# Per-batch statistics one step of attention later, expert weights awaited piece by piece, in a two-layer gated cross-attention and mixture-of-experts kernel

## The chip, the core and the metric

One Trainium2 chip; the kernel runs on one core. The metric is the device time of one execution in microseconds (us). Engines are called PE (TensorE; PEld its weight loads), DVE (VectorE), ACT (ScalarE), POOL (GpSimd) and SP (SyncE, which here issues transfers only).

## The reference, cut to what matters

Two layers, each of cross-attention and a feed-forward part with shared and routed experts. x is 4 batches of 512 tokens by 512; the context has the same tokens by 128. Attention has 32 query heads of 16 columns in 8 groups, one key and value head each. Layer 0 routes to 2 of 8 experts of width 256, layer 1 to 6 of 32 experts of width 192.

```python
def _L0_xattn_ref(q, k, v):            # _L1_xattn_ref computes the same
    QH, KVH = (32, 8); D = E // QH; G = QH // KVH
    qh = q.reshape(b, s, KVH, G, D).transpose(0, 2, 3, 1, 4)
    kh = k.reshape(b, s, KVH, D).transpose(0, 2, 1, 3)
    vh = v.reshape(b, s, KVH, D).transpose(0, 2, 1, 3)
    scores = jnp.einsum('bkgsd,bktd->bkgst', qh, kh) * scale
    attn = jax.nn.softmax(scores, axis=-1) / DROPOUT
    out = jnp.einsum('bkgst,bktd->bkgsd', attn, vh)
...
def _L1_ffn_ref(hidden_states, gate_w, wg, wu, wd, sg, su, sd):
    scores = jax.nn.sigmoid(x @ gate_w)
    topk_w, topk_i = jax.lax.top_k(scores, TOP_K)
    topk_w = topk_w / (jnp.sum(topk_w, axis=-1, keepdims=True) + 1e-20)
    combine = jnp.sum(jax.nn.one_hot(topk_i, N_EXP, dtype=topk_w.dtype) * topk_w[..., None], axis=1)
    g = jnp.einsum('td,edf->tef', x, wg)
    u = jnp.einsum('td,edf->tef', x, wu)
    act = jax.nn.silu(g) * u
    routed = jnp.einsum('tef,efd,te->td', act, wd, combine)
    shared = jax.nn.silu(hidden_states @ sg) * (hidden_states @ su) @ sd
    return routed + shared
x = x + jnp.tanh(g_xattn[0]) * _L0_xattn_ref(_layernorm(x, axis=-1), ctx_512, ctx_512)
x = x + jnp.tanh(g_ffn[0]) * _L0_ffn_ref(_layernorm(x, axis=-1), L0_ffn_w_gate, L0_ffn_w_gate_up, L0_ffn_w_down, L0_ffn_w_sh_gate_up, L0_ffn_w_sh_down)
x = x + jnp.tanh(g_xattn[1]) * _L1_xattn_ref(_layernorm(x, axis=-1), ctx_512, ctx_512)
x = x + jnp.tanh(g_ffn[1]) * _L1_ffn_ref(_layernorm(x, axis=-1), L1_ffn_gate_w, L1_ffn_wg, L1_ffn_wu, L1_ffn_wd, L1_ffn_sg, L1_ffn_su, L1_ffn_sd)
```

## The kernel before, in words

Each engine runs its own program, written out by hand, and engines wait for each other by semaphores. The four parts (attention and feed-forward of layers 0 and 1) follow one another, with a barrier between them. Nothing but the order of the code sets the order of the work.

**Attention** (`make_attention`). All of x (16 tiles of 128 tokens) stays in the memory of the core. A unit is one key head of one batch, with its four query heads; a batch has 8 units (`KVH`), so 32 in all. The function `step(b, k)` exists once for each engine, and step k of batch b does a bit of several units: PE makes scores for the maxima of the next unit (`score_for_max`, L378, into three banks `ring_ps`), DVE reduces each to its maxima (`take_max`, L567, 16 in a step, numbered n = 0 to 15), POOL splits the maxima of the unit before (`split_max`, L246, L249), PE turns them and DVE copies them after reduction 6 (L579), PE makes the scores again with the maxima in them (`score_for_exp`, L395), ACT takes exponentials (L464), PE multiplies by the values (L410), and after reduction 6 DVE also scales the output of an older unit (L588, L592), which POOL adds to x (L277). PE may be as far ahead of DVE as three banks allow. In odd steps PE also turns queries (L337), ACT copies them (L455) and POOL splits them (L263, L266). SP places keys and queries of a unit for PE with seven transfers (`place`, L172 to L181) some steps ahead. In steps 1, 3 and 5 of batch 0 SP loads x and the turned context of the next batch (L148, L145).

The next batch is prepared along the way, by `next_batch` (L513), which DVE calls behind each reduction and which does something behind reductions 0, 4, 8 and 12 (c = 0 to 3). Step 1: one `bn_stats` a place (`moments_of_tile`, L495), the first of which waits for the load of x. Step 2, place 0: four aggregates and an addition (`moments_of_batch`, L500, L503); POOL waits for them at the head of its step 2 and takes the reciprocal root (`root`, L222). Step 3, places 0 and 1: `split_k` (L535), the low part of the keys. Step 4: one `normalize` a place (L508). There is none in the last batch, so that three batches of each layer carry this work.

**Feed-forward** (`make_ffn`). Shared experts first, then routed ones by tiles of 128 gathered rows: 37 tiles in layer 0, 111 in layer 1, ordered by expert. For each tile POOL gathers the rows (L886), PE turns them (L1065), multiplies by gate and up weights (L1077), turns the product (L1088), multiplies by the down weights (L1102), and POOL scatters with an addition (L902). Weights are used in two parts, high and low. SP loads expert e into half e % 2 of two buffers: `w_gu` in two pieces and `w_dn`, each after the piece before has landed (`load_expert`, L767; `expert_w` counts 16 a piece, 48 an expert). ACT rounds to the high part (`gu_hi`, L1238, for each piece; `dn_hi`, L1244), DVE subtracts to get the low part (`gu_lo`, L1537, `dn_lo`, L1622) and so frees the buffer (`gu_split` counts 2 an expert, `dn_split` 1). ACT does this within its steps, between the work on tiles:

```python
                with act.If(late != 0):
                    gu_hi(late, 1)
                silu(i, half)
                h_hi(i - 1, 1 - half)
                x_hi(i + 2, half)
                e = split_of(i)
                with act.If(e != 0):
                    gu_hi(e, 0)
                y_out(i - 2, half)
                with act.If(late != 0):
                    dn_hi(late)
```

## Time and profile before

| | |
|---|---|
| median of 3 runs | 2183.56 us (2182.73 to 2184.03) |
| the profiled execution | 2185.23 us, its span 2183.5 us |
| mean granted clock of PE | 0.965 of full |
| busy: PE | 1980.4 us (91%) |
| busy: DVE | 1367.5 us (63%) |
| busy: ACT | 1086.4 us (50%) |
| busy: POOL | 715.1 us (33%) |
| attention, first to last reduction | 22.6 to 430.4 us (layer 0), 1033.2 to 1441.0 us (layer 1) |

The span goes from the first to the last instruction of one profiled execution. Busy time is that of instructions; a busy PE isn't a PE at its peak. "Idle before" is the time in which an engine had nothing to do ahead of an instruction, and the arrow names what ended it. Start times of adjacent instructions can be closer than their lengths, since they overlap a little. L12 is line 12 of the kernel before.

### The profile page before, as it was taken

How to read it: one execution, taken by the hardware profiler on the slowest of the kernel's cores; microseconds unless marked ns; L12 is line 12 of the kernel's file. 1: busy time of each engine (PE TensorE's matmuls, PEld its weight loads, DVE VectorE, ACT ScalarE, POOL GpSimd, SP SyncE). 2: the span in 40 equal slices, each digit the busy share in tenths (PEclk: the TensorE clock that was granted, in tenths of full speed). 3: DMA queues.
4: the chain of work that ended last, by engine and by line, in shares of the span. 5: the costliest groups of instructions: out<-in, count | busy, mean ns of one | idle time of the engine just before them, and what ended most of it. 6: DMA issues, size and time to landing. Idle time of an engine off the chain costs nothing. (4 is left out here: it accounts for less than half of the span.)

```text
span 2183.5 us, 40476 instructions
## 1 busy us (share of the span) xinstructions
PE 1980.4 (91%) x10072; PEld 1220.5 (56%) x10073; DVE 1367.5 (63%) x2675; ACT 1086.4 (50%) x1673; POOL 715.1 (33%) x848
## 2 busy tenths in 40 slices
PE   4999999979999999993899999988788999999997
PEld 2343333334567657882334333333556888888886
DVE  6898988832234324442889898874876455555553
ACT  1666666741212115541476666662212556666664
POOL 3111211111201005554111121120664555556654
PEclk9999999989999999996799999998999999999998
DMA  4422222151000127765332222204004889988996
GB/s 126 117 55 60 58 62 56 42 191 40 0 1 1 62 83 182 179 109 116 109 86 55 59 65 55 61 11 152 0 1 147 179 184 207 200 197 201 207 207 105
DMA packets 96016, 219.88 MB, mean 101 GB/s; under 512 B 16930, under 2 KB 20004, under 8 KB 95908
## 3 DMA queue, kind: packets, MB, share of 16 engines
q1 hardware_dynamic: 61540, 138.80, 21.6%
q0 software_dynamic: 33792, 79.71, 19.2%
q8 instruction: 59, 0.97, 0.2%
q14 instruction: 49, 0.40, 0.1%
q10 hardware_dynamic: 576, 0.00, 0.0%
HBM read 114.64 MB, written 56.63 MB: 78 GB/s over the span
## 5 line engine op out<-in xcount | busy, mean ns | idle before, releaser
L567 DVE TENSOR_REDUCE maxima<-ring_ps 128x1 f32<-128x512 f32 x1024 | 647.7, 683 | 96.0 <-PE ring_ps L378 95.7
L464 ACT ACTIVATE probs<-score_ps 128x1024 f32<-128x1024 f32 x512 | 503.7, 1025 | 210.6 <-PE score_ps L395 208.8
L378 PE MATMUL ring_ps<-k_turned,q_turned 64*128 64x512 f32 x1024 | 412.5, 481 | 57.9 <-DVE maxima L567 20.3
L378 PEld LDWEIGHTS ring_ps<-k_turned,q_turned 64*128 64x128 f32 x1024 | 176.5, 192 | 374.1 <-DVE maxima L567 232.6
L1077 PE MATMUL bank_f<-w_gu_parts_f,xg_T_f 128*128 x1800 | 368.4, 353 | 1.6 <-issue 1.6
L1077 PEld LDWEIGHTS bank_f<-w_gu_parts_f,xg_T_f 128*128 128x128 f32 x1800 | 327.1, 190 | 30.0 <-issue 2.2
L395 PE MATMUL score_ps<-q_turned,k_turned 64*128 64x512 f32 x1024 | 331.3, 446 | 12.9 <-ACT probs L464 12.8
L410 PE MATMUL out_ps<-probs,v_ones 128*32 128x512 f32 x2048 | 274.5, 608 | 1.8 <-ACT probs L464 1.6
L1102 PE MATMUL bank_f<-w_dn_parts_f,hg_T_f 96*128 (+1 forms) x888 | 243.8, 410 | 2.6 <-DVE hg_T_f L1638 1.4
L902 POOL DMA_INDIRECT out_x<-y_tok_f,idx_out_f x111 | 177.4, 1598 | 139.5 <-ACT y_tok_f L1276 109.7
L886 POOL DMA_INDIRECT xg_f<-xh_rows_f,idx_in_f x156 | 159.8, 1025 | 183.3 <-DVE idx_in_f L1528 118.4
L1020 PE MATMUL bank_f<-x_parts_f,w_sh_parts_f 128*128 128x512 f32 x792 | 205.7, 401 | 0.0
L1047 PE MATMUL bank_f<-w_sh_down_f,h_T_f 128*128 128x512 f32 x352 | 163.2, 614 | 12.6 <-DVE h_T_f L1572 7.6
L1102 PEld LDWEIGHTS bank_f<-w_dn_parts_f,hg_T_f 96*128 96x128 f32 (+1 forms) x888 | 158.1, 190 | 28.6 <-issue 3.5
L395 PEld LDWEIGHTS score_ps<-q_turned,k_turned 64*128 64x128 f32 x1024 | 148.8, 186 | 40.2 <-ACT probs L464 31.2
L1020 PEld LDWEIGHTS bank_f<-x_parts_f,w_sh_parts_f 128*128 128x128 f32 x792 | 149.6, 190 | 33.4 <-issue 2.4
L863 POOL TENSOR_SCALAR slot_hot_f<-count_f_f,slot_of_f 128x128 fp32r<-128x128 f32 x128 | 103.7, 816 | 185.9 <-PE bank_f L999 184.3
L263 POOL CAST q_hi<-q_raw 128x512 fp32r<-128x512 f32 x30 | 18.4, 615 | 361.8 <-ACT q_raw L455 287.8
L277 POOL TENSOR_TENSOR x_res<-x_res,scaled 128x256 f32<-128x256 f32 x64 | 47.1, 737 | 240.0 <-DVE scaled L592 240.0
L1047 PEld LDWEIGHTS bank_f<-w_sh_down_f,h_T_f 128*128 128x128 f32 x352 | 67.9, 196 | 92.9 <-issue 76.3
L1537 DVE TENSOR_TENSOR w_gu_parts_f<-w_gu_f,w_gu_parts_f (+2 forms) x80 | 80.5, 1011 | 61.9 <-ACT w_gu_parts_f L1238 59.9
L1632 DVE TENSOR_TENSOR xg_T_f<-bank_f,xg_T_f 128x512 fp32r<-128x512 f32 x152 | 104.0, 685 | 15.6 <-ACT xg_T_f L1251 12.3
(210 smaller groups left out, 2213.1 us busy)
## 6 DMA issues: line engine op xcount, KB each, us to landing
w_gu_f<-in_L_w_gu SPq DMA_DIRECT2D x64, 384.0 KB
q_turned<-q_hi SPq DMA_DIRECT2D x128, 128.0 KB, 2.6
w_dn_f<-in_L_w_dn SPq DMA_DIRECT2D x32, 384.0 KB
k_turned<-k_hi SPq DMA_DIRECT2D x128, 64.0 KB, 2.1
q_turned<-no_max SPq DMA_DIRECT2D x64, 128.0 KB, 2.6
q_turned<-q_lo SPq DMA_DIRECT2D x64, 128.0 KB, 2.6
xh_rows_f<-xh_f SPq DMA_DIRECT2D x8, 1024.0 KB, 9.0
w_gu_f<-in_L_w_gu SPq DMA_DIRECT2D x16, 512.0 KB
```

Of the source, the lines that this page charges most:

```text
L378: pe.matmul(ring(k, "max", i), q_turned[rows, slot, h // 2, c * P:(c + 1) * P], k_turned[rows, slot, :], start=True, stop=True).then_inc(m ...
L395: mm = pe.matmul(score_ps[:, pair, a, :], k_turned[rows, slot, c * P:(c + 1) * P], q_turned[rows, slot, pair, :], start=True, stop=True)
L410: mm = pe.matmul(out_ps[32 * h:32 * h + 32, :], v_ones[:, (k - LAG_EXP) % RING, c, :], probs[:, c % 2, h // 2, h % 2, :], start=(c == 0), ...
L464: act.activation(probs[:, c % 2, pair, :, :], score_ps[:, pair, :, :], ACT.Exp, scale=float(D) ** -0.5).then_inc(exped, 1)
L567: dve.tensor_reduce(maxima[:, par, col:col + 1], ring(k, "max", i), AX.X, ALU.max).then_inc(max_taken, 1)
L886: pool.indirect_dma_start(xg[:, half, :], None, xh_rows, bass.IndirectOffsetOnAxis(ap=idx_in[:, half:half + 1], axis=0)).then_inc(gathered ...
L902: pool.indirect_dma_start(acc_rows, bass.IndirectOffsetOnAxis(ap=idx_out[:, half:half + 1], axis=0), y_tok[:, half, :], None, compute_op=A ...
L1020: mm = pe.matmul(bank[:, 2 * (n % NBK) + o, :], w_sh_parts[:, o, w_part, d, :], x_parts[:, x_part, d, :], start=(d == 0 and j == 0), stop= ...
L1047: mm = pe.matmul(bank[:, 6 + c % 2, :], h_T[:, f, c * P:(c + 1) * P], w_sh_down[:, f, :], start=(f == 0), stop=(f == FC - 1))
L1077: mm = pe.matmul(bank[:, half, 0:2 * F], xg_T[:, half, x_part, d, :], w_gu_parts[:, bass.ds(par, 1), w_part, d, :].rearrange("p a f -> p ( ...
L1102: mm = pe.matmul(bank[:, 2 + half, :], hg_T[:, half, h_part, f, :], w_dn_parts[:, bass.ds(par, 1), w_part, f, :].rearrange("p a f -> p (a ...
L1632: dve.tensor_tensor(xg_T[:, half, 1, :, :].rearrange("p d m -> p (d m)"), bank[:, 6, :], xg_T[:, half, 0, :, :].rearrange("p d m -> p (d m ...
```

## The change

The statistics of the next batch move from step 1 to step 2, its aggregates from step 2 to step 3, with POOL's root; the two splits of the keys stay in step 3 but come behind reductions 4 and 8 where they came behind 0 and 4. In the loop over experts, SP waits for the split of piece 0, piece 1 and the down weights of the expert before last each ahead of the load that overwrites it, where it waited for all three ahead of the first. ACT's rounding of a piece waits until that piece has landed, where it waited for the whole expert, and the rounding of the down weights has a wait of its own.

```diff
--- before.py
+++ after.py
@@ -284,7 +284,7 @@
             pool.tensor_scalar(ctx_tok[:], ctx_tok[:], gate[:, 0:1], None, ALU.mult).then_inc(v_gated, 1)
 
             def step(b, k):
-                if k == 2 and b < B - 1:
+                if k == 3 and b < B - 1:
                     root(b + 1)
                 split_max(b, k)
                 if isinstance(b, int) and b == 0 and k == LAG_MAX:
@@ -515,14 +515,14 @@
                 c, rest = divmod(n, 4)
                 if b + 1 >= B or rest:
                     return
-                if k == 1:
+                if k == 2:
                     if c == 0:
                         dve.wait_ge(x_loaded[b + 1], 16)
                     moments_of_tile(b + 1, c)
-                elif k == 2 and c == 0:
+                elif k == 3 and c == 0:
                     moments_of_batch(b + 1)
-                elif k == 3 and c < 2:
-                    split_k(b + 1, c)
+                elif k == 3 and c < TPB - 1:
+                    split_k(b + 1, c - 1)
                 elif k == KVH // 2:
                     if c == 0:
                         dve.wait_ge(ln_rstd, b + 2)
@@ -767,10 +767,18 @@
             def load_expert(e, half):
 
                 for piece in range(2):
+                    if not isinstance(e, int):
+
+                        sp.wait_ge(gu_split, 2 * e + (piece - 3))
+                        sp.nop(nofuse=True)
                     rows, n = slice(piece * HC // 2, (piece + 1) * HC // 2), HC * F
                     sp.dma_start(w_gu[:, half, rows, :].rearrange("p c f -> p (c f)"),
                                  t["w_gu"](e)[:, :, piece * n:(piece + 1) * n].rearrange("a p n -> p (a n)")).then_inc(expert_w, 16)
                     sp.wait_ge(expert_w, 48 * e + (16 * piece + 16))
+                    sp.nop(nofuse=True)
+                if not isinstance(e, int):
+
+                    sp.wait_ge(dn_split, e - 1)
                     sp.nop(nofuse=True)
                 sp.dma_start(w_dn[:, half, :, :].rearrange("p c h -> p (c h)"), t["w_dn"](e).rearrange("a p n -> p (a n)")
                              ).then_inc(expert_w, 16)
@@ -800,11 +808,6 @@
                     e = pair * 2 + half
 
                     sp.wait_ge(expert_w, 48 * e)
-                    sp.nop(nofuse=True)
-
-                    sp.wait_ge(gu_split, 2 * e - 2)
-                    sp.nop(nofuse=True)
-                    sp.wait_ge(dn_split, e - 1)
                     sp.nop(nofuse=True)
                     load_expert(e, half)
             turns = sp.value_load(turns_i[0:1, 0:1], min_val=4, max_val=64)
@@ -1232,7 +1235,7 @@
 
             def gu_hi(e, piece):
 
-                act.wait_ge(expert_w, 48 * e + 48)
+                act.wait_ge(expert_w, 48 * e + (16 * piece + 16))
                 par = e % 2 if isinstance(e, int) else act.snap(e % 2)
                 rows = slice(piece * HC // 2, (piece + 1) * HC // 2)
                 act.activation(w_gu_parts[:, bass.ds(par, 1), 0, rows, :].rearrange("p a d f -> p (a d f)"),
@@ -1240,6 +1243,7 @@
                                ).then_inc(gu_hi_done, 1)
 
             def dn_hi(e):
+                act.wait_ge(expert_w, 48 * e + 48)
                 par = e % 2 if isinstance(e, int) else act.snap(e % 2)
                 act.activation(w_dn_parts[:, bass.ds(par, 1), 0, :, :].rearrange("p a f h -> p (a f h)"),
                                w_dn[:, bass.ds(par, 1), :, :].rearrange("p a f h -> p (a f h)"), ACT.Copy).then_inc(dn_hi_done, 1)
```

DVE, steps 0 to 2 of batch 0 in layer 0 (and the start of step 3). `maxima<-ring_ps` is a reduction, `stats` the statistics, `mean_var` the aggregates. Before:

```order
L567 TENSOR_REDUCE maxima<-ring_ps 128x1 x5
L495 BN_STATS stats<-x_res 128x6
L567 TENSOR_REDUCE maxima<-ring_ps 128x1 x4
L495 BN_STATS stats<-x_res 128x6
L567 TENSOR_REDUCE maxima<-ring_ps 128x1 x4
L495 BN_STATS stats<-x_res 128x6
L567 TENSOR_REDUCE maxima<-ring_ps 128x1 x4
L495 BN_STATS stats<-x_res 128x6
L567 TENSOR_REDUCE maxima<-ring_ps 128x1 x4
L500 BN_AGGR mean_var<-stats 128x2 x4
L503 TENSOR_SCALAR mean_var<-mean_var 128x4
L567 TENSOR_REDUCE maxima<-ring_ps 128x1 x6
```

Now:

```order
L567 TENSOR_REDUCE maxima<-ring_ps 128x1 x21
L495 BN_STATS stats<-x_res 128x6
L567 TENSOR_REDUCE maxima<-ring_ps 128x1 x4
L495 BN_STATS stats<-x_res 128x6
L567 TENSOR_REDUCE maxima<-ring_ps 128x1 x2
L579 CAST max_rows<-ring_ps 32x128
L567 TENSOR_REDUCE maxima<-ring_ps 128x1 x2
L495 BN_STATS stats<-x_res 128x6
L567 TENSOR_REDUCE maxima<-ring_ps 128x1 x4
L495 BN_STATS stats<-x_res 128x6
L567 TENSOR_REDUCE maxima<-ring_ps 128x1 x4
L500 BN_AGGR mean_var<-stats 128x2 x4
```

The reduction behind which the first `stats` comes is now the 21st and no longer the fifth: the four sit in step 2, on both sides of the copy of the maxima, and the aggregates follow reduction 0 of step 3.

POOL, from step 1 of batch 0 on, with what each waits for; `rstd` is the root. Before:

```order
L263 CAST q_hi<-q_raw 128x512 [waits attn_q_copied]
L266 TENSOR_TENSOR q_lo<-q_raw,q_hi 128x512 [waits attn_q_hi_made]
L222 TENSOR_TENSOR rstd<-mean_var,minus_half 128x4 [waits attn_ln_var]
L246 CAST max_parts<-maxima 128x16 [waits attn_max_taken]
L249 TENSOR_TENSOR max_parts<-maxima,max_parts 128x16 [waits attn_max_hi]
L234 COPY v_ones<-ctx_tok 128x4x16
L246 CAST max_parts<-maxima 128x16 [waits attn_max_taken]
```

Now:

```order
L263 CAST q_hi<-q_raw 128x512 [waits attn_q_copied]
L266 TENSOR_TENSOR q_lo<-q_raw,q_hi 128x512 [waits attn_q_hi_made]
L246 CAST max_parts<-maxima 128x16 [waits attn_max_taken]
L249 TENSOR_TENSOR max_parts<-maxima,max_parts 128x16 [waits attn_max_hi]
L234 COPY v_ones<-ctx_tok 128x4x16
L222 TENSOR_TENSOR rstd<-mean_var,minus_half 128x4 [waits attn_ln_var]
L246 CAST max_parts<-maxima 128x16 [waits attn_max_taken]
```

The root has moved behind one more split of the maxima, and stands now ahead of the split in step 3, a step in which queries are split too.

SP, the second half of the loop over experts in layer 0. Before:

```order
L805 ISA [waits ffn_expert_w]
L771 ISA [waits ffn_gu_split,ffn_dn_split]
L771 DMA w_gu_f<-in_L_w_gu 128x1024
L773 REGISTER_ALU
L771 ISA [waits ffn_expert_w]
L771 DMA w_gu_f<-in_L_w_gu 128x1024
L773 REGISTER_ALU
L775 ISA [waits ffn_expert_w]
L775 DMA w_dn_f<-in_L_w_dn 128x1024
```

Now:

```order
L772 ISA [waits ffn_expert_w]
L775 ISA [waits ffn_gu_split]
L775 DMA w_gu_f<-in_L_w_gu 128x1024
L777 REGISTER_ALU
L772 REGISTER_ALU [waits ffn_expert_w]
L775 ISA [waits ffn_gu_split]
L775 DMA w_gu_f<-in_L_w_gu 128x1024
L777 REGISTER_ALU
L783 ISA [waits ffn_expert_w,ffn_dn_split]
L783 DMA w_dn_f<-in_L_w_dn 128x1024
```

The load of the first piece no longer stands behind the split of the down weights (`ffn_dn_split`); this wait is now ahead of the load of the down weights.

## Rows read from the trace of the kernel before

**Rows 1.** The page, part 1: busy time and share of the span.
```profile
PE 1980.4 (91%) x10072; PEld 1220.5 (56%) x10073; DVE 1367.5 (63%) x2675; ACT 1086.4 (50%) x1673; POOL 715.1 (33%) x848
```

**Rows 2.** Windows by step: length; PE, PEld, DVE, ACT, POOL busy; clock; DMA; GB/s.
```profile
24.96:43.16 18.20, 10.89 (x21) 4.78 (x20) 12.21 (x22) 1.54 (x2) 1.88 (x2) 1.00 0.41 134
131.74:145.24 13.50, 12.81 (x79) 5.55 (x79) 13.00 (x23) 8.95 (x11) 2.60 (x3) 1.00 0.24 61
145.24:157.50 12.26, 11.46 (x75) 4.88 (x75) 11.15 (x25) 8.47 (x10) 2.91 (x8) 1.00 0.22 54
157.50:171.00 13.50, 12.77 (x79) 5.42 (x79) 11.87 (x21) 8.95 (x11) 2.74 (x4) 1.00 0.13 34
171.00:183.46 12.46, 12.02 (x75) 4.96 (x71) 12.35 (x23) 8.62 (x10) 1.98 (x6) 1.00 0.36 87
335.74:348.89 13.15, 12.26 (x79) 5.09 (x79) 10.84 (x19) 8.94 (x11) 2.74 (x4) 1.00 0.28 70
348.89:360.90 12.01, 11.41 (x75) 4.71 (x73) 10.78 (x20) 8.47 (x10) 1.73 (x6) 1.00 0.21 52
1035.62:1054.03 18.41, 10.89 (x21) 4.78 (x20) 12.20 (x21) 2.82 (x3) 1.88 (x2) 0.50 0.41 134
1054.03:1065.02 10.99, 9.96 (x24) 5.01 (x23) 10.39 (x23) 2.02 (x2) 2.20 (x7) 0.50 0.16 40
1065.02:1079.48 14.46, 13.08 (x70) 4.96 (x70) 11.36 (x21) 8.91 (x11) 2.45 (x5) 0.88 0.49 153
```

**Rows 3.** Timeline of DVE, layer 0, step 1 of batch 0: start, length, what, [idle before].
```profile
30.54 0.69 DVE L495 BATCH_NORM_STATS2 stats<-x_res 128x6 f32<-128x512 f32 x1 [4.91 <-DMA x_res<-in_x]
```

**Rows 4.** Timeline of DVE, layer 1, the same place.
```profile
1041.42 0.69 DVE L495 BATCH_NORM_STATS2 stats<-x_res 128x6 f32<-128x512 f32 x1 [5.13 <-DMA x_res<-acc_rows_f]
```

**Rows 5.** Waits of PE, 1675 to 2170 us: total, times, longest.
```profile
PE bank_f L1065 <- DMA xg_f<-xh_rows_f,idx_in_f: 2.7, 2, 2.3
PE bank_f L1065 <- DVE xg_T_f L1632: 2.3, 1, 2.3
PE bank_f L1102 <- DVE hg_T_f L1638: 1.4, 1, 1.4
```

**Rows 6.** Waits of SP's queue, 1675 to 2170 us.
```profile
SPq L808 <- DVE w_dn_parts_f L1622: 25.1, 11, 3.9
SPq L806 <- DVE w_gu_parts_f L1537: 8.5, 3, 3.6
```

**Rows 7.** Timeline of DVE, layer 0, batch 1, steps 1, 2 and 4.
```profile
132.34 0.68 DVE L495 BATCH_NORM_STATS2 stats<-x_res 128x6 f32<-128x512 f32 x1
132.94 2.46 DVE L567 TENSOR_REDUCE maxima<-ring_ps 128x1 f32<-128x512 f32 x4
135.33 0.68 DVE L495 BATCH_NORM_STATS2 stats<-x_res 128x6 f32<-128x512 f32 x1
...
145.85 0.37 DVE L500 BATCH_NORM_AGGREGATE mean_var<-stats 128x2 f32<-128x6 f32 x4
...
146.33 3.07 DVE L567 TENSOR_REDUCE maxima<-ring_ps 128x1 f32<-128x512 f32 x5
...
150.54 0.27 DVE L579 CAST max_rows<-ring_ps 32x128 fp32r<-32x128 f32 x1
...
151.35 3.15 DVE L567 TENSOR_REDUCE maxima<-ring_ps 128x1 f32<-128x512 f32 x5
...
174.46 0.54 DVE L508 TENSOR_SCALAR xh<-x_res,mean_var,rstd 128x512 f32<-128x512 f32 x1
174.91 1.45 DVE L567 TENSOR_REDUCE maxima<-ring_ps 128x1 f32<-128x512 f32 x2
```

**Rows 8.** Timeline of ACT, layer 1, rounding of an expert's piece 0.
```profile
1962.33 0.85 ACT L1238 ACTIVATE w_gu_parts_f<-w_gu_f  x1 [2.36 <-DMA w_dn_f<-in_L_w_dn]
```

**Rows 9.** Chain of waits, layer 1, a gather in the expert loop.
```profile
1708.99 6.22 DMA xg_f<-xh_rows_f,idx_in_f
```

**Rows 10.** Timeline of SP's queue, the load of weights at that place.
```profile
1709.88 6.21 SPq L771 DMA_DIRECT2D w_gu_f<-in_L_w_gu  x2
```

## The prediction

> **What bounds the kernel now.** I read the page first, then the run cut by step of attention, then the timelines of the places that the diff touches, then the tables of waits. On the page TensorE (PE) is busy for 91% of the span [rows 1]; so work moved between other engines shows only where PE waits for them. The slices don't tell where, so I cut the attention of both layers into steps of one head, from the first reduction of one step to that of the next (a step issues 16 reductions on VectorE, DVE) [rows 2]. The reader is to see three kinds. In the last batch, which prepares no other, an odd step takes 13.15 us (it also turns queries) and an even one 12.01, with DVE busy for 10.8: PE sets these. Step 4 of a middle batch, with four normalizations added, takes 12.46 and DVE is busy for 12.35: DVE sets it. Step 1 of batch 0 takes 18.20 in layer 0 and 18.41 in layer 1, with DVE busy for 12.2 of it: something makes both wait. The timeline of DVE names it: before the first `stats` of batch 1 it stands 4.91 us for the load of x, in layer 1 5.13 us [rows 3, 4]. No scores are exponentiated yet there, PE has only the scores for the maxima to make, and its three banks are full as soon as DVE stops. This wait is on the path.
>
> For the experts I read what PE waits for in the expert stage of layer 1. Three waits, 5.0 us in all, have to do with gathered tokens, and 1.4 us with the down projection's input; no row there names the gate-up matmul waiting for weights [rows 5]. So the weights' rounding is in time already, though SyncE (SP), which issues the loads, stood 25.1 us for the split of down weights and 8.5 us for that of gate-up weights [rows 6].
>
> **The change part by part.** A chip measurement of this kernel can tell some 0.2%, 4.4 us, from no change.
>
> *Statistics, batch 0.* Step 1 loses the wait and four `stats`; step 2 gains the four. The data landed when DVE went on, at 30.54 and 1041.42 [rows 3, 4]. In the changed kernel they are wanted at the start of step 2. Step 1 then lasts about 18.20 less 4.91 less four spacings of 0.60 (start to start in [rows 7]: 132.34 to 132.94, which is what a `stats` costs a DVE that is never idle), 10.9 us; from 24.96 that is 35.9, over 5 us after the landing. In layer 1 it is 1046.5, also 5 us after. The whole wait goes: 4.91 + 5.13 = 10.04. The four `stats` cost 2.4 in step 1 and 2.4 in step 2, both paced by DVE, and cancel. The aggregates (four and an addition, 145.85 to 146.33, 0.48 us [rows 7]) leave step 2, paced by DVE, for step 3, where PE paces; there I charge what they cost in a PE-paced step of a middle batch, 12.26 less 12.01, 0.25. That is 0.23 less per layer. Batch 0 gives 10.04 + 0.46 = **10.5 us less**.
>
> *Batches 1 and 2, twice over two layers.* Step 1 took 13.50 with `stats` in it and takes 13.15 without: 0.35 less. Step 2 is the one that the trace does not show: four `stats` in an even step. Its DVE work, at the spacings of [rows 7], is 16 reductions (132.94 to 135.33 is four, so 0.60 each) 9.6, the turned maxima, reciprocal and scaling 0.81 (150.54 to 151.35), and four `stats` 2.4: 12.8, over PE's 12.01. The same sum for step 4, with four normalizations of 0.45 (174.46 to 174.91), gives 12.2 against 12.46 measured, so 0.2 more is lost to hand-overs. I take 13.0, or 0.74 more than the 12.26 of now. The bounds are 12.46, the step with the lighter addition, and 14.4, where nothing is hidden (12.01 + 2.4); 13.0 is nearest to the first because PE-paced steps do hide most of such work. Step 3 had two key splits and 13.50; it now has the aggregates at reduction 0 and the splits at 4 and 8. Four `stats` at 0, 4, 8 and 12 cost an odd step no more than two splits at 0 and 4 (13.50 both), so a late place costs nearly nothing, and a split at 0 or 4 some 0.18. New step 3: 13.15 + 0.25 + 0.18 = 13.58, 0.08 more; bounds 0 and 0.5. Together 0.74 + 0.08 − 0.35 = 0.47 more per batch, four times: **1.9 us more** (bounds 0 and 7).
>
> *The square root on GpSimd (POOL)* moves with the aggregates, and stands in front of that step's `split_max`, which PE's turning of the maxima waits for. In step 2 it did the same and cost PE no more than the 0.25 charged above. Queries are split in odd steps, behind it, but they come only after reduction 10, more than 4 us later. Normalization asks for the root one step later, in step 4, and the root is still some 10 us early. SP's placing of the next batch's keys asks for both splits; the second comes four reductions, 2.4 us, later, ahead of a placing that is used only in the next batch: nothing.
>
> *Experts.* SP may load piece 0 of an expert when piece 0 of the one before last is split, not when its down weights are; ScalarE (ACT) may round piece 0 when it has landed. The clearest case: ACT stood 2.36 us at 1962.33 for down weights that this rounding does not read [rows 8]. That wait goes. But PE has no wait in [rows 5] that weights end; what hides all this is one tile of slack between rounding and use, so I charge **0**. The new waits of SP sit ahead of loads only; its queue holds nothing else in the loop. If the cover were gone, the 2.36 us is the most that one expert could show. Bounds: 3 us less, if a little over half of the 5.0 us of token waits goes because ACT is earlier; 3 us more, if moved loads meet gathers and make one more wait like the longest of [rows 5], 2.3 us.
>
> **Sum.** −10.5 + 1.9 + 0 = −8.6 us. Against the profiled execution, 2185.23 (span 2183.5), that is 2176.6; that execution stands 1.7 over the median of the runs shown, 2183.56, and the forecast for the median is **2174.9**, 0.39% less.
>
> **A rule weighed.** PE's clock in layer 1 is at 0.50 of full (1.2 GHz) through steps 1 and 2 of batch 0 and at full for most of step 3 (0.88), although PE is busy for 9.96 of 10.99 us of step 2 [rows 2]. I therefore leave it out of the sum: steps 1 and 2 are paced by DVE at either level. The Trainium skill, "TensorE: Matmul & The Clock Gate", Part 1, says that the clock starts halved and that sustained activity releases it; by that rule a step 1 without a hole could release it a step sooner. By the rows what this could give is what step 3 of batch 0 lasts over a full-clock step with the same work, 14.46 less 13.50: 1.0 us a layer.
>
> **The rivals.**
> 1. *The clock rises sooner.* Without the hole PE is fed evenly through step 1. For it: the clock does rise soon after PE has dense work. Against: at 91% busy in step 2 it had not risen. 2.0 us less: 2172.9. Chance 0.10.
> 2. *Step 2 becomes DVE's, dearly.* The three banks hide less than in step 4 and the loss carries into step 3: 14.0 for step 2 and 13.9 for step 3, 1.3 more for each of four batches, 5.3 us: 2180.2. Against: step 4 shows nearly pure DVE time. Chance 0.08.
> 3. *Another wait takes the place of the first.* Step 1 gets shorter by 7 us, and PE wants the next heads' queries and keys, placed by SP's transfers, sooner. These are issued ahead of and behind the same load of x. Price up to 5 us a layer if they land as late as x did; 2184.9, no change. Against: head 2's scores are wanted only 12 reductions into step 2, over 7 us after x has landed. Chance 0.04.
> 4. *The expert loads collide with the gathers, and the kernel is slower than before.* Earlier loads run beside the gathers that PE waits for. A gather issued at 1708.99 with a load of weights 0.9 us behind it landed 6.2 us later [rows 9, 10], and PE stood 2.3 us for it, the longest such wait of [rows 5]. SP was held by splits 14 times in layer 1 [rows 6], and each of these loads moves. If every one met a gather so, 14 × 2.3 = 32 us, less the 8.6: 2207. It decides from the sixth such wait on (six times 2.3 is 13.8, over 8.6 + 4.4). Against: gathers have two tiles of lead, and most loads run beside one already. The Trainium skill's "DMA: Bandwidth & Descriptors", Issuing engines are not separate DMA queues, says that all issuing engines' transfers share the same 16 engines; the late landing at 1708.99 agrees. Chance 0.05.
> 5. *The piece-wise waits do shorten the expert stage* as they are meant to, through ACT and the scatters behind it, by 3 us: 2171.9. Chance 0.06.
>
> The forecast as it stands has 0.67.
>
> **How the numbers follow.** The forecast's own spread is the bounds of step 2 and step 3 used in part (1 less to 3 more) and the experts' jitter (2 either way): 2172.5 to 2177.5. The range reaches to rivals 1 and 5 below and most of the way to 2 above: 2171.3 to 2179.3. Faster by over 0.2% means under 2179.2: the forecast, rivals 1 and 5, and a small part of rival 2, 0.85. Within 0.2%: the rest of 2, rival 3 and mild cases of 4, 0.11. Slower: 0.04.
>
> **What would show it.** Right: no wait of DVE for x at step 1 of batch 0 in either layer, and that step near 11 us; step 2 of batch 0 near 12.9; in batches 1 and 2 steps 1, 2 and 3 near 13.15, 13.0 and 13.6; ACT's 2.36 us gone with the expert stage's length the same within 2 us. Wrong: step 2 of the middle batches over 13.5, a wait for placed queries at batch 0, or more and longer waits of PE for gathered tokens.

## The result and the profile after

| | before | after |
|---|---|---|
| median (5 runs each, on one chip) | 2183.56 us (2178.90 to 2187.91) | 2170.13 us (2169.02 to 2174.77) |
| ratio to before, 95% interval | | 0.9935 [0.9909, 0.9962] |
| the profiled execution, its span | 2185.23 us, 2183.5 us | 2170.13 us, 2168.4 us |
| mean granted clock of PE | 0.965 | 0.967 |

The change saves 13.4 us where 8.6 were forecast: 2170.13 against 2174.9, and 1.2 us below the low end of the range. The sign was right, the size was not. The profile after, page part 1, answers to [rows 1]; the work of each engine is as before to 0.3%, so the gain is in waits and in the clock.

```profile
PE 1977.3 (91%) x10072; PEld 1216.8 (56%) x10073; DVE 1369.0 (63%) x2675; ACT 1087.0 (50%) x1673; POOL 713.8 (33%) x848
```

**Attention by step.** The same windows as [rows 2] (length; PE, PEld, DVE, ACT, POOL busy; clock; DMA; GB/s): steps 1 and 2 of batch 0 in layer 0, steps 1 to 4 of batch 1, steps 1 to 3 of batch 0 in layer 1.

```profile
24.81:35.70 10.89, 10.27 (x21) 4.71 (x20) 9.74 (x17) 1.54 (x2) 2.09 (x4) 1.00 0.65 222
35.70:48.20 12.50, 10.63 (x24) 5.00 (x23) 12.31 (x22) 2.05 (x2) 0.34 (x2) 1.00 0.23 54
125.80:138.95 13.15, 12.27 (x79) 5.10 (x79) 10.84 (x19) 8.96 (x11) 2.74 (x4) 1.00 0.25 64
138.95:151.82 12.87, 12.49 (x75) 5.16 (x71) 12.84 (x23) 8.77 (x11) 1.14 (x3) 1.00 0.23 58
151.82:165.21 13.39, 12.68 (x78) 5.67 (x79) 12.32 (x27) 8.75 (x10) 4.30 (x8) 1.00 0.11 27
165.21:177.67 12.46, 12.02 (x75) 4.97 (x71) 12.35 (x24) 8.63 (x10) 1.98 (x6) 1.00 0.37 88
1023.91:1034.80 10.89, 10.27 (x21) 4.71 (x20) 9.74 (x17) 2.83 (x3) 2.09 (x4) 0.50 0.66 223
1034.80:1047.30 12.50, 10.63 (x24) 5.01 (x23) 12.31 (x22) 2.05 (x2) 0.33 (x2) 0.50 0.23 53
1047.30:1064.32 17.02, 16.45 (x70) 6.06 (x70) 11.90 (x25) 8.87 (x10) 4.05 (x9) 0.64 0.37 117
```

Step 1 of batch 0 fell from 18.20 to 10.89 us, in layer 1 from 18.41 to the same. In the middle batches step 1 lost its 0.35, step 2 went from 12.26 to 12.87 and is now DVE's (busy 12.84 of it), and step 3 went from 13.50 to 13.39. One row is worse than before: step 3 of batch 0 in layer 1 took 17.02 us at a mean clock of 0.64, where [rows 2] have 14.46 at 0.88.

**The wait for x.** The timeline of DVE from step 1 of batch 0 on, in layer 0 (start, length, what, idle before):

```profile
28.77 3.68 DVE L567 TENSOR_REDUCE maxima<-ring_ps 128x1 f32<-128x512 f32 x6 [0.29 <-PE ring_ps L378]
33.30 3.08 DVE L567 TENSOR_REDUCE maxima<-ring_ps 128x1 f32<-128x512 f32 x5 [0.86 <-PE ring_ps L378]
36.30 0.68 DVE L495 BATCH_NORM_STATS2 stats<-x_res 128x6 f32<-128x512 f32 x1
36.90 2.46 DVE L567 TENSOR_REDUCE maxima<-ring_ps 128x1 f32<-128x512 f32 x4
```

And the same place in layer 1:

```profile
1035.40 0.68 DVE L495 BATCH_NORM_STATS2 stats<-x_res 128x6 f32<-128x512 f32 x1
```

The first `stats` now starts at 36.30 with nothing waited for; in [rows 3] it waited 4.91 us, in [rows 4] 5.13. What is left of idle DVE time in step 1 is PE's (0.29 and 0.86).

**Experts, layer 1.** The tables of waits of PE and of SP's queue, 1659 to 2155 us, beside [rows 5] and [rows 6] (total, times, longest):

```profile
PE bank_f L1068 <- DMA xg_f<-xh_rows_f,idx_in_f: 2.8, 3, 1.2
PE bank_f L1068 <- DVE xg_T_f L1636: 2.3, 1, 2.3
PE bank_f L1105 <- DVE hg_T_f L1642: 1.4, 1, 1.4
```

```profile
SPq L773 <- DVE w_gu_parts_f L1541: 35.3, 10, 9.4
```

PE's waits are those of before, with the 2.7 us for gathers now 2.8, in three pieces of at most 1.2 instead of one of 2.3 and a short one. SP waits for the split of down weights no longer at all (25.1 us in eleven before); it stands 35.3 us for gate-up pieces instead, where the two waits of before together were 33.6, since it now comes there earlier.

**Stage by stage.** To compare runs I cut each profiled execution at five places, from the starts and ends of the same instructions: attention (first to last reduction), and the expert stage (first turned tile of gathered rows to the last down matmul), in each layer. Between them lie normalization, the router and the shared experts, which the change does not touch. Microseconds:

| | attention 0 | shared 0 | experts 0 | attention 1 | shared 1 | experts 1 | span |
|---|---|---|---|---|---|---|---|
| before | 407.8 | 375.7 | 191.2 | 407.8 | 234.8 | 499.2 | 2183.5 |
| after | 402.3 | 372.6 | 188.1 | 404.8 | 233.6 | 499.9 | 2168.4 |
| change, e3 | 402.4 | 372.7 | 189.2 | 402.5 | 235.2 | 500.9 | 2169.6 |
| change, e12 | 404.9 | 374.4 | 191.8 | 404.8 | 233.6 | 498.9 | 2175.2 |
| attention alone, e1 | 402.4 | 375.2 | 192.2 | 404.8 | 233.6 | 502.2 | 2177.8 |
| attention alone, e10 | 402.3 | 375.6 | 191.3 | 404.7 | 233.6 | 500.8 | 2175.9 |
| experts alone, e2 | 408.6 | 374.0 | 187.6 | 407.9 | 233.3 | 501.3 | 2180.6 |
| experts alone, e9 | 407.6 | 374.0 | 188.7 | 408.0 | 234.9 | 502.0 | 2181.8 |
| e4 | 403.3 | 375.6 | 188.9 | 403.0 | 233.8 | 502.2 | 2173.8 |
| e5 | 402.1 | 375.5 | 188.6 | 402.3 | 232.2 | 501.0 | 2168.9 |
| e6 | 402.4 | 372.3 | 189.6 | 402.4 | 235.1 | 500.8 | 2170.5 |
| e7 | 401.8 | 372.6 | 189.1 | 402.1 | 232.2 | 500.0 | 2165.0 |
| e8 | 401.7 | 373.8 | 189.0 | 401.1 | 233.0 | 502.0 | 2168.2 |
| e11 | 404.4 | 374.0 | 188.9 | 402.2 | 232.9 | 500.0 | 2170.1 |

Of the 15.1 us between the two spans, 8.5 are attention, 3.1 are the experts of layer 0, 4.3 are shared stages whose code is the same, and the experts of layer 1 give 0.7 back. These shared stages move by up to 3.4 us from run to run with the same code, so a difference of one profiled execution to another says nothing below that; the experiments are read by their timed ratios and by stages. Much of this scatter is one fall of the clock: between 540 and 556 us its mean is 0.89 in eight of the executions, whose first shared stage lasts 373.8 to 375.7 us, and 1.00 in six, with 372.3 to 374.0. The kernel before as profiled has the fall, the kernel after has not, and e12, the same kernel as the latter, has it.

### The profile page after: what moved, and what is told of

Its sections match the earlier page's. It is cut to its first block and busy times, and to the rows that moved or that the text cites. A ratio compares the mean times of both kernels' runs of the same rounds, so it can differ in the third digit from the quotient of the medians.

```text
span 2168.4 us, 40585 instructions
## 1 busy us (share of the span) xinstructions
PE 1977.3 (91%) x10072; PEld 1216.8 (56%) x10073; DVE 1369.0 (63%) x2675; ACT 1087.0 (50%) x1673; POOL 713.8 (33%) x848
## 5 line engine op out<-in xcount | busy, mean ns | idle before, releaser
L378 PE MATMUL ring_ps<-k_turned,q_turned 64*128 64x512 f32 x1024 | 417.1, 484 | 46.2 <-DVE scaled L592 16.3
L395 PE MATMUL score_ps<-q_turned,k_turned 64*128 64x512 f32 x1024 | 335.7, 449 | 13.0 <-ACT probs L464 13.0
```

Source lines behind the costliest of these rows:

```text
L378: pe.matmul(ring(k, "max", i), q_turned[rows, slot, h // 2, c * P:(c + 1) * P], k_turned[rows, slot, :], start=True, stop=True).then_inc(m ...
L395: mm = pe.matmul(score_ps[:, pair, a, :], k_turned[rows, slot, c * P:(c + 1) * P], q_turned[rows, slot, pair, :], start=True, stop=True)
```

## The experiments

The medians of the kernel before, one for each group of runs on one chip, were 2185.28 us (23 runs; e1 to e4), 2187.04 (12; e5 to e7), 2186.30 (17; e8 to e10) and 2186.77 (11; e11, e12). Each is 1.7 to 3.5 us over the 2183.56 of the forecast, and single executions lay between 2179 and 2194. Two theories stood at the start: that attention alone gives the whole gain, or that the experts' part gives a share of it.

**1. Attention alone** (e1, and again as e10): the change with SP and ACT of the expert loop as before.

```diff
                 for piece in range(2):
-                    if not isinstance(e, int):
-
-                        sp.wait_ge(gu_split, 2 * e + (piece - 3))
-                        sp.nop(nofuse=True)
...
-                act.wait_ge(expert_w, 48 * e + (16 * piece + 16))
+                act.wait_ge(expert_w, 48 * e + 48)
```

> The attention part of the change alone, on the kernel before. Theory 1 (the statistics' wait was the gain, the experts' part gives nothing, and the rest of the measured gain is clock dips and gather waits that differ from execution to execution): 8 to 10 us less than before, about 2174, and the time of the whole change within its scatter. Theory 2 (the piece-wise waits give what the forecast lacked): 8 to 10 us less here, clearly above the whole change by 4 to 6 us.

> The attention part of the change alone, a second time, beside the run above. Theory 1 (the experts' part is worth nothing): as fast as the whole change, 12 to 13 us less than before. Theory 2 (the whole is the sum of the two parts): 8 to 11 us less than before, the layer 0 stage of the experts 191 to 192 us with one wait of 2 to 2.6 us for gathered rows, layer 1 with one such wait of about 2.5 us. Attention itself as in the change: batch 0 10.9, 12.5 and 14.7 us by step, the middle batches 13.15, 12.87, 13.39 and 12.46.

Measured: e1 2176.95 us (6 runs), ratio 0.9953 [0.9937, 0.9969]; e10 2174.81 us (6 runs), ratio 0.9957 [0.9943, 0.9970]. That is 10.3 and 9.4 us less by ratio.

**2. Experts alone** (e2, and again as e9): attention as before, the expert loop as in the change.

```diff
...
-                if k == 2:
+                if k == 1:
                     if c == 0:
                         dve.wait_ge(x_loaded[b + 1], 16)
                     moments_of_tile(b + 1, c)
-                elif k == 3 and c == 0:
+                elif k == 2 and c == 0:
                     moments_of_batch(b + 1)
-                elif k == 3 and c < TPB - 1:
-                    split_k(b + 1, c - 1)
+                elif k == 3 and c < 2:
+                    split_k(b + 1, c)
```

> The experts' part of the change alone. Theory 1: the time of before within 1.5 us; SyncE's wait for the down weights' split is gone, PE's expert stages are as long as before. Theory 2: 4 to 6 us less, about 2178, with the gain inside the two expert stages and mostly in layer 0, where the profile of the whole change is 3.1 us shorter.

> The experts' part of the change alone, a second time, to tell what it is worth by itself. Theory 1 (it is worth nothing, the first run's difference was scatter): the ratio to before holds 1, 0.9995 to 1.0005 in the middle; TensorE waits for the gathered rows of layer 0 for 2 us or more in one piece. Theory 2 (earlier weight loads leave the gather of the next tokens free): 2 to 3 us less than before (ratio 0.9985 to 0.999), the stage of layer 0 from the first turned rows to the last down matmul 187.5 to 189.5 us where before took 191.2, and no wait for gathered rows over 2 us in it; in layer 1 the first wait for gathered rows in pieces of under 1.6 us where before had 2.3 in one.

Measured: e2 2184.24 us (11 runs), ratio 0.9990 [0.9977, 1.0002]; e9 2182.33 us (12 runs), ratio 0.9985 [0.9970, 0.9999]. That is 2.2 and 3.3 us less. Each alone is at the edge of no effect; both lie on the same side.

**3. The whole change again** (e3, e12).

> The whole change once more, to see what repeats. Both theories: attention of layer 0 again 5.7 us shorter, steps of the middle batches again 13.15, 12.87 and 13.39. Theory 1: the clock dips of the feed-forward part of layer 0 and the step of 17.0 us in layer 1 come out otherwise, and the median lies between 2170 and 2175. Theory 2: the expert stage of layer 0 again 3 us shorter.

> The change itself, a third time, as the partner of the run above. 12 to 15 us less than before (ratio 0.9930 to 0.9945) if the parts add up to the whole; the profiled span 2168 to 2171 us, the layer 0 stage of the experts 188 to 189.2 us.

Measured: e3 2172.67 us (6 runs), ratio 0.9942 [0.9925, 0.9959]; e12 2171.55 us (6 runs), ratio 0.9920 [0.9905, 0.9934]. The three ratios of the change have a mean of 0.9932, 14.8 us; the two parts multiplied (0.9955 × 0.9988) give 0.9943, 12.5 us. So the parts add up to the whole within the intervals, and by these ratios about a fifth of it is the experts'. The profiled execution of e12 missed what was expected of it: its span was 2175.2 us and its stage of layer 0 191.8, for the reason shown next.

What the experts' part does is best seen some 40 us into the expert stage of layer 0. The timeline of PE there, in e10 (attention alone), and then the window of 4 us from that instruction on:

```profile
844.19 1.11 PE L1065 MATMUL bank_f<-ident,xg_f 128*128 128x128 f32 x4 [2.41 <-DMA xg_f<-xh_rows_f,idx_in_f]
```

```profile
844.19:848.19 4.00, 4.00 (x13) 3.39 (x14) 2.02 (x5) 1.86 (x4) 0.99 (x1) 0.58 1.01 238
```

The same two in e9 (experts alone):

```profile
846.82 0.66 PE L1068 MATMUL bank_f<-ident,xg_f 128*128 128x128 f32 x4 [1.13 <-DMA xg_f<-xh_rows_f,idx_in_f]
```

```profile
846.82:850.82 4.00, 4.00 (x20) 3.41 (x21) 2.12 (x5) 2.52 (x5) 0.99 (x1) 1.00 0.98 252
```

And in e12, the whole change:

```profile
846.11 1.11 PE L1068 MATMUL bank_f<-ident,xg_f 128*128 128x128 f32 x4 [2.25 <-DMA xg_f<-xh_rows_f,idx_in_f]
```

```profile
846.11:850.11 4.00, 4.00 (x13) 3.39 (x14) 2.02 (x5) 1.85 (x4) 0.99 (x1) 0.58 0.95 238
```

The wait for one gather is there in nearly all kernels, and at this place the clock fell behind it where it lasted over 2 us: PE is busy for the whole 4 us in each window, but gets through 13 matmuls at 0.58 where it gets through 20 at 1.00. Such a fall costs another 4 × 0.42 = 1.7 us. Over the 14 profiled executions: with SP loading as before the longest such wait was 2.05 (before), 2.53 (e1), 2.41 (e10), 1.85 (e4) and 1.77 (e6), and the clock fell in the first three; with SP loading by pieces it was 1.09, 1.83, 0.95, 1.30, 0.70, 1.13, 1.33, none over 0.2 in e2, and 2.25 with the fall in e12. The stage took 191.2 to 192.2 us in the four executions with the fall and 187.6 to 189.6 in the ten without. Its mean is 190.6 with the loads as before (five) and 189.0 with the pieces (nine); PE's waits for gathers in it have a mean of 2.5 and 1.4 us, and the falls (1.7 us each, three in five against one in nine) account for the rest.

The same place in layer 1, 34 to 40 us into its stage, bears out the shorter waits but not that 2 us decide the fall. With the loads as before PE waits there once, for 2.31 us (before), 2.61 (e1, e4), 2.73 (e10) and 2.38 (e6); with the pieces its longest in the whole stage is 1.10 to 1.96 in all nine. But the clock fell behind 1.88 us in e12 and 1.96 in e8, and did not fall behind the 2.31 of the kernel before, here with the 4 us from that instruction on:

```profile
1715.25 0.66 PE L1065 MATMUL bank_f<-ident,xg_f 128*128 128x128 f32 x4 [2.31 <-DMA xg_f<-xh_rows_f,idx_in_f]
```

```profile
1715.25:1719.25 4.00, 4.00 (x23) 3.70 (x24) 1.68 (x5) 1.40 (x3) 1.49 (x3) 1.00 1.04 259
```

So the length of the wait alone does not decide it. In sum PE waits 2.6 us a stage for gathers in layer 1 with either order of loads, only in other pieces, and the stage has a mean of 501.0 and 500.7: no difference that counts.

The queues in e10 and e9 show where the loads moved. SP's queue, e10 (the gather that PE waited for was issued at 836.62 or 840.66):

```profile
837.96 7.20 SPq L771 DMA_DIRECT2D w_gu_f<-in_L_w_gu  x2
```

SP's queue, e9 (gathers at 834.06 and 839.84):

```profile
835.76 5.16 SPq L775 DMA_DIRECT2D w_gu_f<-in_L_w_gu  x2
```

Counted from the start of the stage (800.5 and 804.2) the two pieces of gate-up weights go out from 37.5 and from 31.6 us on, 5.9 us earlier. This holds in every execution: 37.1 to 38.1 in the five with the loads as before, e6 with its rounding by pieces among them, and 31.0 to 32.5 in the nine others. In this stage SP stood 9.9 us in five waits for splits of down weights in e10 and not at all in e9. The longest gather took 7.5 us from issue to landing in e10 and 6.9 in e9. That the gathers land sooner because the two pieces are further along is my reading of these rows; no run held a load back to test it, and in e12, with the first piece at 31.3, a gather took 7.8 us all the same.

**4. Loading x earlier instead** (e4): the kernel before, with SP's loads of the next x and context in steps 0, 2 and 4.

```diff
-                if b == 0 and k % 2 and k // 2 + 1 < B:
+                if b == 0 and k % 2 == 0 and k // 2 + 1 < B:
```

> The kernel before, with SyncE's loads of the next batch's x and context one step earlier (steps 0, 2 and 4 of batch 0) and the statistics where they were. If the gain of the attention part is the wait for x, the wait goes here too: step 1 of batch 0 lasts 13.3 instead of 18.2 us in both layers, 10 us less in all, about 2173.5, though nothing is moved on DVE. If it is the place of the statistics among the reductions, nothing is gained. A risk for both: the placing of head 1 is issued 1.2 us later, and PE may wait for it.

Measured: 2178.78 us (12 runs), ratio 0.9972 [0.9960, 0.9985], 6.1 us less. DVE's timeline in e4:

```profile
26.19 0.69 DVE L495 BATCH_NORM_STATS2 stats<-x_res 128x6 f32<-128x512 f32 x1 [0.54 <-DMA x_res<-in_x]
```

With 0.54 of the 4.91 us left, step 1 of batch 0 takes 13.84 us and step 2 its old 10.99; step 1 gets shorter by the wait and by nothing else (18.20 − 13.84 = 4.36 against 4.91 − 0.54 = 4.37; in layer 1 4.53 against 5.13 − 0.59 = 4.54). So the wait is on the path one for one, as the prediction read it. The change saves 5.8 a layer over the first three steps, 1.4 more than layer 0 gains here: 0.5 is what is left of the wait in e4, and 0.9 is that step 2 grows by 1.5 only, where the four `stats` cost 2.4 in step 1: the aggregates leave it, and the `stats` fill time in which DVE was idle. The timed gain is less than expected, 6.1 us for 10; the two steps alone give 8.9, just outside the interval (3.3 to 8.7). The one profiled execution has 9.3 us less in attention than before; its time, 2175.50, is 3.3 us below the median of e4, and I don't know which executions lose what it kept.

**5. Which half of the experts' part** (e5: attention and SP's loads by pieces, ACT as before; e6: attention and ACT's rounding by pieces, SP as before).

```diff
--- change
+++ e5
-                act.wait_ge(expert_w, 48 * e + (16 * piece + 16))
+                act.wait_ge(expert_w, 48 * e + 48)
...
--- change
+++ e6
-                        sp.wait_ge(gu_split, 2 * e + (piece - 3))
...
+                    sp.wait_ge(gu_split, 2 * e - 2)
+                    sp.nop(nofuse=True)
+                    sp.wait_ge(dn_split, e - 1)
```

> The attention part and, of the experts' part, the loads alone: SyncE waits piece by piece, ScalarE waits for the whole expert as before. So far the profiles without the experts' part have PE wait 1.85 to 2.53 us for a gather some 40 us into layer 0's expert stage, and 2.3 to 2.6 us in one wait early in layer 1's; those with it 0 to 1.83 us, and two shorter waits. If the earlier loads did that: as in the whole change here (layer 0's expert stage 188 to 189 us, two shorter waits in layer 1), 2171 to 2174 in all. If the earlier rounding did: as in the attention part alone (191 to 192 us, one wait of 2.5 us in layer 1), 2174 to 2177.

> The attention part and, of the experts' part, ScalarE's piece-wise waits alone: SyncE waits for all three splits ahead of the first load, as before. If the earlier loads moved PE's waits for gathers: one wait of 1.8 to 2.6 us in each layer's expert stage as before, 2174 to 2177. If the earlier rounding did: no such wait in layer 0 or a shorter one, and two shorter ones in layer 1, 2171 to 2174. ScalarE's wait of 2.36 us for down weights at a rounding of piece 0 is gone in either case.

Measured: e5 2174.89 us (6 runs), ratio 0.9949 [0.9931, 0.9966]; e6 2176.74 us (7 runs), ratio 0.9957 [0.9941, 0.9973]. The two intervals overlap over most of their length, and each reaches to attention alone: time does not tell the halves apart. Nor does the stage of layer 0, 188.6 in e5, 189.6 in e6 and 188.9 in e4, which has neither half, nor the count of falls there: three in five executions against one in nine, whether they are sorted by the loads or by the rounding. The waits do, by the sign that both expectations named. PE at the gather in layer 1, in e6 (loads as before) and in e5 (loads by pieces; its other wait is 1.15 too):

```profile
1699.98 0.66 PE L1065 MATMUL bank_f<-ident,xg_f 128*128 128x128 f32 x4 [2.38 <-DMA xg_f<-xh_rows_f,idx_in_f]
```

```profile
1698.80 0.66 PE L1068 MATMUL bank_f<-ident,xg_f 128*128 128x128 f32 x4 [1.15 <-DMA xg_f<-xh_rows_f,idx_in_f]
```

In layer 0 the longest wait is 1.77 in e6 and 0.95 in e5. So it is the loads that shorten PE's waits for gathers; what that is worth in time, these runs don't resolve. ACT's wait of 2.36 us of [rows 8] went with either half (the longest wait for weights ahead of a rounding in layer 1 is 2.4 before and 2.6 in e1, but 0.9 in e5 and in e6), and gave nothing that a stage shows: in sum ACT stands 9.5 us for weights there before and after, and the mean of layer 1 is 501.1 with the rounding as before and 500.6 by pieces.

**6. Statistics late in both steps** (e7, and again as e11): two `stats` in step 1 and two in step 2, each behind reductions 8 and 12.

```diff
-                if k == 2:
-                    if c == 0:
+                if k == 1 and c >= 2:
+                    if c == 2:
                         dve.wait_ge(x_loaded[b + 1], 16)
+                    moments_of_tile(b + 1, c - 2)
+                elif k == 2 and c >= 2:
                     moments_of_tile(b + 1, c)
```

> The whole change, with the statistics spread: two in step 1 and two in step 2, each behind reductions 8 and 12. If what an addition costs in a step that PE paces depends on its place (0 and 4 dear, 8 and 12 nearly free), the middle batches' steps 1, 2 and 3 last 13.15, 12.1 and 13.4 us where the change has 13.15, 12.87 and 13.39, 0.77 less in each of four batches; batch 0 may wait up to 0.3 us for x in step 1. Together 2.5 us less than the change in the attention steps. If the number of additions counts whatever their place, steps 1 and 2 last 13.35 and 12.4 us, 0.3 less a batch, 1.1 us in all.

> The change with two of the four statistics in step 1 and two in step 2, each behind reductions 8 and 12, a second time and beside the change on one chip. Theory A (statistics late in an odd step cost nothing, in an even one 0.24 us each): middle batches 13.15, 12.50, 13.40, that is 0.36 us less than the change in each of four, batch 0 0.3 us more per layer: 1.5 us less less 0.6, so 0.5 to 1.5 us under the change below. Theory B (the first run's 2169.4 was scatter): within 0.5 us of the change or over it, with the same step lengths as the change in its sum.

Windows of steps 1 to 3 of batch 1 in e7:

```profile
125.86:139.02 13.16, 12.28 (x79) 5.21 (x79) 11.97 (x21) 8.95 (x11) 2.72 (x4) 1.00 0.25 64
139.02:151.52 12.50, 11.96 (x75) 4.86 (x73) 11.79 (x21) 8.76 (x11) 1.13 (x3) 1.00 0.24 60
151.52:164.92 13.40, 12.68 (x78) 5.67 (x79) 12.33 (x27) 8.74 (x10) 4.30 (x8) 1.00 0.11 28
```

Two `stats` late in step 1 cost 0.01 us in all; two in step 2 cost 0.49 over the 12.01 of [rows 2], 0.25 each, where 12.1 was expected for the whole step. Measured: e7 2169.42 us (6 runs), ratio 0.9925 [0.9908, 0.9941]; e11 2172.29 us (6 runs), ratio 0.9921 [0.9901, 0.9940]. Beside e12 on the same chip (0.9920) it is no faster. The steps gain the 0.37 per middle batch that they should, 1.5 in all less 0.6 for batch 0, and timing can't see 0.9 us. It beats the kernel before, and is not shown to beat the change.

**7. All statistics late in step 1** (e8): behind reductions 9, 11, 13 and 15.

```diff
+                if b + 1 < B and k == 1 and n >= 9 and n % 2:
+                    if n == 9:
+                        dve.wait_ge(x_loaded[b + 1], 16)
+                    moments_of_tile(b + 1, (n - 9) // 2)
...
```

> The change, but the four statistics of the next batch all stand in step 1, behind reductions 9, 11, 13 and 15, and none in step 2. Theory A (one statistics operation costs nothing in a step that TensorE paces, and about 0.24 us in a step where the reductions nearly pace): in the middle batches step 1 stays at 13.15 to 13.35 us, step 2 falls from 12.87 to about 12.0, step 3 stays at 13.39; some 0.7 to 0.85 us less for each of eight middle batch turns less the ones before the last, so 4 to 5 us less in all against the change (2165 to 2169 us against a before of 2183 to 2186), batch 0's wait for the next x in step 1 at most 0.5 us. Theory B (statistics late in step 1 delay its last banks): step 1 at 13.5 to 14.0 us, and the sum of steps 1 and 2 as in the change, 25.9 to 26.0 us; time as the change's, 2170 to 2173 us.

Windows of steps 1 and 2 of batch 1 in e8:

```profile
126.24:139.95 13.71, 12.85 (x82) 5.38 (x80) 12.99 (x23) 9.47 (x12) 3.14 (x6) 1.00 0.25 61
139.95:151.93 11.98, 10.99 (x73) 4.52 (x72) 10.78 (x21) 7.96 (x9) 0.73 (x1) 1.00 0.23 56
```

Measured: 2168.01 us (6 runs), ratio 0.9929 [0.9908, 0.9950]. Both theories missed in part. Step 2 is at 11.98 as theory A has it, step 1 at 13.71 as theory B has it: four late `stats` close together cost 0.56, more than the 0.35 that the four spread ones cost before, where two cost nothing. The two steps sum to 25.69, against 26.02 in the change, 25.66 in e7 and 25.76 before, where step 2 also had the aggregates. By its interval (10.9 to 20.1 us less than before) e8 is not told from the change either.

## Why the prediction was right and wrong

- **Batch 0 (forecast −10.5): right in kind, 1.1 us too small.** The wait went whole in both layers, as read from [rows 3, 4], and step 1 came out at 10.89 for a forecast of 10.9. Step 2 took 12.50, not 12.9, and the aggregates cost step 3 nothing where 0.25 was charged. Its length hangs on when the clock rises, so steps have to be compared that rise alike: the third score matmul took 585 ns in layer 1 before and in layer 0 of e5, and these steps lasted 14.46 and 14.45. The failed step is "The four `stats` cost 2.4 in step 1 and 2.4 in step 2, both paced by DVE, and cancel": in [rows 2], step 2 took 10.99 with DVE busy for 10.39, so 0.6 of it was free, and the `stats` filled 0.4 of that (12.31 busy of 12.50 now). Three steps of batch 0 give 5.8 less a layer, 11.6 in all.
- **The middle batches (forecast +1.9): the term was mis-sized by 1.3.** Step 2 was taken at 13.0 and is 12.87; its DVE time (12.84) is the sum of spacings, 12.8, and the 0.2 added for hand-overs is not there. Step 3 was charged 0.08 more and got 0.11 less: the aggregates at reduction 0 and the splits at 4 and 8 together cost 0.24 over an odd step that prepares nothing, where 0.43 was charged by adding their single prices. The upper bound of 7 was also added up wrong: with 14.4 for step 2 and 0.5 for step 3 it is 4 × (2.14 + 0.5 − 0.35) = 9.2. Nothing came near it. Together (13.15 + 12.87 + 13.39) − (13.50 + 12.26 + 13.50) = 0.15, four times: +0.6.
- **The experts (forecast 0): the largest miss, about 2 us.** That PE has no wait that weights end still holds, and rounding earlier gave nothing that PE's waits show. What failed is to charge 0 because "The new waits of SP sit ahead of loads only". The loads share time with gathers that PE waits for, and the prediction saw only the harm of that (rival 4). PE's waits for gathers got shorter with them (2.5 to 1.4 us in layer 0): the mean of both expert stages is 2.0 us shorter (1.6 and 0.3, rounded), the timed ratios of experts alone say 2.2 and 3.3. Rival 5, at 2171.9, is nearest to the measured time, but that is luck: it had the gain come through ACT and the scatters, while in e5 and e6 PE's waits get shorter with the loads and not with ACT's rounding.
- **The clock (left out of the sum; rival 1): the opposite of what rival 1 said.** It held that a step 1 without a hole might bring the full clock sooner. It can come later. In step 3 of batch 0 PE runs at half clock first and then at full, and the switch came within the first 5 us or after some 12. The timeline of PE in layer 1, the same eight matmuls with the values some 7 us into step 3, in the change as profiled first:

```profile
1054.12 1.93 PE L410 MATMUL out_ps<-probs,v_ones 128*32 128x512 f32 x8
```

  and in e3:

```profile
1054.97 1.07 PE L410 MATMUL out_ps<-probs,v_ones 128*32 128x512 f32 x8
```

  The first took 1.93 us, the second 1.07, with the same work ahead of both. Step 3 lasts 17.02 against 14.68. The late place appeared in 5 of the 14 such steps that have the change's attention (layer 1 of the profile after, e1, e10, e12; layer 0 of e12), once more in e11, and in none of the eight of kernels with the statistics as before (one of them, in e2, took 15.4: it rose early, fell back to half some 6 us into the step and rose again). Whether the change makes it likelier, or this is chance, is open. It takes back 2.35 us each time, on average 5/14 × 2 × 2.35 = 1.7 us of the whole; the prediction left the clock out of the sum, and had it in a rival only as a gain. The Trainium skill, "TensorE: Matmul & The Clock Gate", Part 1, says that sustained activity releases the clock; the trace agrees in that layer 1 starts at 0.50 and rises under work, but with PE busy for 10.27 of 10.89 us in step 1, where it had been for 10.89 of 18.41 [rows 2], the rise still did not come before step 3.
- **The sum.** −11.6 + 0.6 + 1.7 − 2.0 = −11.3 by the profiles, and attention alone by the means of the stages: 806.4 for seven executions against 815.9 for three, −9.5 (timed: −9.4 and −10.3). Timed, the whole change gave 12.7, 14.2 and 17.5 us by its three ratios. The 1 to 6 us between −11.3 and these three are not explained; the shared stages scatter by as much, and whether they have a part in it that is due to the change wasn't settled.
- **The chances.** 0.85 on faster was fair. The range was too narrow at its low end. Its own spread, 1 us less on the steps and 2 on the experts, reaches 2171.9 if both fall the same way, and the range ended close by, at 2171.3, with batch 0 given no spread at all. Three terms fell the same way: 1.1, 1.3 and 2.0 add to 4.4, of which the clock took back 1.7. That the time ended only 1.2 us outside the range is partly owed to that.

## What to carry to other kernels

Read the step that an operation leaves and the one that it enters for idle time of its own engine: an addition fills what is free there before it costs anything. Single prices do not add: spread additions cost less than their sum here, and crowded ones more than spread ones. A wait of the engine that empties a small ring of buffers was on the path one for one, and removing it gave more than all moves of the work around it. When transfers move, ask for gains as well as for harm from those that they no longer meet, and judge gains below 3 us by repeated timings and by many stages, not by two profiles.

## What the runs showed of the hardware that was not expected

In the expert stages PE's waits for a gather of 1.88 to 2.73 us were followed by some 4 us at a mean clock of 0.50 to 0.70 in ten cases, and one of 2.31 us was not (layer 1 before, 1.00); none of 1.85 us or less was. In the clearest pair, layer 0 of e10 and of e9, waits of 2.41 and 1.13 us were followed by 13 and by 20 matmuls in 4 us. With the same instructions ahead of it the full clock came early or late in step 3 of batch 0 (matmuls are at full by 4.9 us into it in e3, and still at half at 10.3 us in the profile after, layer 1): the step took 14.1 to 14.7 us or 16.9 to 17.2 (15.4 once), and what decides between the two is not shown here. In layer 0 the granted clock reads 1.00 all through (step 3 of e12 too, 17.18 us long), and only the durations of the matmuls show the half clock there. In a step paced by PE through three banks, four `stats` behind every second reduction cost 0.56 us, behind every fourth 0.35, and two behind reductions 8 and 12 nothing. So it counts how close together they stand; no run had two at the early places, so that the place itself matters too isn't ruled out.
